# A graph kernel's first hop: the last step's look-ups issued within that step, its matches and marks two tiles a slot, one list step less

## The reference

```python
def _spmm(edge_src, edge_dst, edge_weight, feats, n_nodes):
    msgs = edge_weight[:, None] * feats[edge_src]
    return jax.ops.segment_sum(msgs, edge_dst, num_segments=n_nodes)
feats = [x]; cur = x
for _ in range(n_blocks - 1):            # n_blocks = 4
    cur = _spmm(edge_src, edge_dst, edge_weight, cur, n_nodes)
    feats.append(cur)
gnn = jnp.concatenate(feats, axis=1) @ shared_weight + output_bias
out = _layernorm(x + gnn)                # over the 256 features, eps 1e-5
```

## Time and profile before

| | us |
|---|---|
| three runs of the kernel | 1563.99, 1564.5, 1565.31 (median 1564.5) |
| the profiled execution, its own time | 1565.78 |
| its span on the core | 1563.8 |
| PE busy in the span | 1421.7 (91%) |
| DVE busy | 1193.1 (76%) |
| ACT busy | 1077.0 (69%) |
| POOL busy | 1068.9 (68%) |
| DMA, mean over the span | 286 GB/s |

### The profile page before, as it was taken

The page is one execution under the profiler, slowest core; times in us unless marked ns, Lnnn a source line. Parts: engine busy times, 40 slices in busy tenths (PEclk is TensorE's granted clock), DMA queues, the critical chain, the costliest instruction groups (busy, mean ns, idle before and its releaser), DMA issues. The chain is left out here.

```text
span 1563.8 us, 31224 instructions
## 1 busy us (share of the span) xinstructions
PE 1421.7 (91%) x7970; PEld 1194.6 (76%) x7970; DVE 1193.1 (76%) x4909; ACT 1077.0 (69%) x2674; POOL 1068.9 (68%) x1043
## 2 busy tenths in 40 slices
PE   7999999999999977499989999898889888899993
PEld 5888888888888855388868877777767776677882
DVE  6877777777777768678754443699999999999773
ACT  4777777777777743368855554577777877788774
POOL 4577777777777754657746666357777777777764
PEclk9999999999999989799999999999999999999996
DMA  7889899989998989589978777799999999999862
GB/s 260 280 288 293 294 312 306 304 293 290 308 305 295 308 289 342 178 296 366 369 267 198 172 188 173 226 304 333 321 337 326 336 323 325 335 338 328 298 223 92
DMA packets 221960, 446.52 MB, mean 286 GB/s; under 512 B 30622, under 2 KB 136297, under 8 KB 221787
## 3 DMA queue, kind: packets, MB, share of 16 engines
q1 hardware_dynamic: 171462, 337.11, 62.8%
q0 software_dynamic: 49328, 106.72, 23.4%
q10 hardware_dynamic: 996, 0.72, 0.2%
HBM read 227.00 MB, written 225.94 MB: 290 GB/s over the span
## 5 line engine op out<-in xcount | busy, mean ns | idle before, releaser
L1392 PE MATMUL ps_y<-w_sb,xT 128*128 128x256 f32 x2640 | 696.1, 389 | 26.9 <-DVE y_ring L1716 13.8
L1392 PEld LDWEIGHTS ps_y<-w_sb,xT 128*128 128x128 f32 x2640 | 472.1, 194 | 93.8 <-ACT xT L1104 26.1
L1117 ACT ACTIVATE o_ring<-y_ring,shift,rstd 128x256 f32<-128x256 f32 (+1 forms) x782 | 422.3, 590 | 0.0
L1716 DVE TENSOR_TENSOR y_ring<-ps_y,bias 128x512 f32<-128x512 f32 x391 | 268.5, 687 | 136.9 <-PE ps_y L1392 113.9
L1722 DVE BATCH_NORM_STATS2 stats<-y_ring 128x6 f32<-128x256 f32 (+1 forms) x782 | 290.8, 413 | 3.7
L857 POOL DMA_INDIRECT rows_in<-in_x,gather_idx x200 | 201.3, 1007 | 87.2 <-issue 63.9
L857 POOL DMA_INDIRECT tails_found<-tail_keys,table_idx x200 | 200.2, 1001 | 81.5 <-issue 58.8
L861 POOL DMA_INDIRECT out_rows<-u_out,tailo_idx x197 | 202.2, 1026 | 74.2 <-issue 48.5
L857 POOL DMA_INDIRECT rows_in<-out_rows,tailx_idx x160 | 166.9, 1043 | 84.6 <-issue 37.1
L1476 PE MATMUL ps_u<-w_sb,cT 128*128 128x256 f32 x788 | 206.2, 384 | 0.0
L1381 PE MATMUL ps_xT<-ident,x_ring 128*128 128x128 f32 x1196 | 185.8, 279 | 15.8 <-ACT xT L1104 9.8
(11 more groups left out here) (283 smaller groups left out, 2231.6 us busy)
## 6 DMA issues: line engine op xcount, KB each, us to landing
x_ring<-in_x SPq DMA_DIRECT2D x195, 512.0 KB
out_rows<-o_ring SPq DMA_DIRECT2D x195, 512.0 KB, 4.7
c_rows<-zeros SPq DMA_DIRECT2D x50, 512.0 KB
c_rows<-sums SPq DMA_DIRECT2D x49, 512.0 KB
u_rows<-u_out SPq DMA_DIRECT2D x49, 512.0 KB
keys_bc<-u_rows SPq DMA_DIRECT2D x25, 512.0 KB, 7.1
tails_found<-u_rows SPq DMA_DIRECT2D x12, 512.0 KB, 7.7
listed<-u_rows SPq DMA_DIRECT2D x12, 512.0 KB, 6.6
```

The costliest lines, as they stand in the source:

```text
L1117: last = act.activation(o_ring[slot][0:rows, r * D:(r + 1) * D], y_ring[k][0:rows, r * D:(r + 1) * D], ACT.Identity, bias=shift[k][0:rows, ...
L1392: last = pe.matmul(ps_y[p % 2][0:rows, r * D:(r + 1) * D], columns_of(p)[0][:, q * P:q * P + rows], w_sb[:, c, :], start=c == 0, stop=c == ...
L1716: dve.tensor_tensor(y_ring[k][0:rows, half * 2 * D:(half + 1) * 2 * D], ps_y[half][0:rows, :], bias2[0:rows, :], ALU.add).then_inc(y_copie ...
```

## The change

The look-ups of a-step 24 are issued by POOL within a-step 24, one after each look-up of step 23, and land in buffers of their own (`last_found`, slices of the two key buffers that are free by then), counted on the semaphores `list_in[0]` and `list_in[1]`. For that DVE makes their table index in slot 3 of a-step 24, and ACT counts the tiles of step 24 beside those of step 23, in a-step 23 (two sign operations a slot, none in a-step 24). DVE matches both step 23's and step 24's tiles in list step 0 (two a slot, step 23 in slots 0 to 3), and marks both in list step 1. So `LIST0` is 3 instead of 4: there are nine list steps, and the step behind the head, list step 3, carries two dense units. SP fills four tables of zeros a list step instead of three from list step 1 on; the store of `listed` comes in list step 2, and the rows gathered ahead are stored in list step 3, behind it.

```diff
--- before.py
+++ after.py
@@ -51,11 +51,11 @@
     A_UNIT = STEP
     A_STEPS = TILES // Q
     LIST_UNIT = A_UNIT + PAIR * A_STEPS
-    LIST0 = 4
+    LIST0 = 3
     LIST_STEPS = 5
     LIST_ALL = LIST0 + LIST_STEPS + 1
     ONE = 1
-    B_UNIT = LIST_UNIT + ONE * LIST_ALL + STEP
+    B_UNIT = LIST_UNIT + ONE * LIST_ALL + ONE + STEP
     B_STEPS = LIST_STEPS
     BRIDGE_UNIT = B_UNIT + FOUR * B_STEPS
     FIRST_GROUPS = 2 * LIST_STEPS
@@ -246,6 +246,7 @@
 
         half_keys = [keys_bc[0][:, 0:G * P], keys_bc[0][:, G * P:Q * P], keys_bc[1][:, 0:G * P]]
         half_segments = [t.bitcast(u8)[:, 0:G * P] for t in half_keys]
+        last_found = [keys_bc[1][:, (q + 1) * P:(q + 2) * P] for q in range(Q - 1)] + [keys_bc[0][:, P:2 * P]]
         own_c2 = [u_out[:, k, :] for k in range(G)]
         v_out = [u_out[:, G + k, :] for k in range(G)]
         u_in = [t.rearrange("p (k d) -> p k d", d=D) for t in
@@ -459,7 +460,8 @@
             return A_UNIT + PAIR * i, PAIR, turns, STEP if isinstance(turns, int) and i == 0 else PAIR
 
         def list_step(l):
-            return LIST_UNIT + ONE * l, ONE, 0, PAIR
+            size = [PAIR if i == LIST0 else ONE for i in range(LIST_ALL)]
+            return LIST_UNIT + sum(size[:l]), size[l], 0, size[l - 1] if l > 0 else PAIR
 
         def b_step(b):
             return B_UNIT + FOUR * b, FOUR, 0, FOUR if b > 0 else STEP
@@ -502,7 +504,7 @@
 
         def list_count(m, groups):
 
-            return 16 * G * groups + (16 * G * A_STEPS if m >= 2 else 0)
+            return 16 * G * groups + (16 * G * (A_STEPS - 1) if m >= 2 else 16 * G)
 
         def tile_rows(table, t, n):
 
@@ -639,19 +641,19 @@
                 zero_c2(zeroed + k)
             zeroed += 3
             for l in range(1, LIST_ALL):
-                if l == 2:
+                if l == LIST0 - 1:
+                    sp.wait_ge(listed_copied, A_STEPS)
+                    sp.dma_start(list_dram.rearrange("(p t) f -> p (t f)", p=P),
+                                 listed[:, :, :].rearrange("p t f -> p (t f)")).then_inc(tables_stored, 16)
+                if l == LIST0:
 
                     for k in range(Q):
                         q = (AHEAD0 + k) % Q
                         sp.wait_ge(tailx_in[q], 16)
                         sp.dma_start(ahead_dram[k * P:(k + 1) * P, :], rows_in[q][:, :]).then_inc(rows_ready, 16)
-                if l == LIST0 - 1:
-                    sp.wait_ge(listed_copied, A_STEPS)
-                    sp.dma_start(list_dram.rearrange("(p t) f -> p (t f)", p=P),
-                                 listed[:, :, :].rearrange("p t f -> p (t f)")).then_inc(tables_stored, 16)
                 if l < LIST_ALL - 1:
                     store_and_load(list_step(l))
-                    for k in range(3):
+                    for k in range(4):
                         if zeroed < ZERO_FILLS:
                             zero_c2(zeroed)
                             zeroed += 1
@@ -879,6 +881,12 @@
                 limit(SLOTS)
                 gather(tails_found[:, q, :], tail_keys_dram, table_idx[k][:, q:q + 1], table_done[q // G])
 
+            def look_up_last(q):
+                if q == 0:
+                    pool.wait_ge(table_staged, A_STEPS)
+                    limit(SLOTS)
+                gather(last_found[q], tail_keys_dram, table_idx[(A_STEPS - 1) % 3][:, q:q + 1], list_in[q // G])
+
             def step_a(a, dense, place):
                 last = isinstance(a, int) and a == A_STEPS - 1
                 if isinstance(a, int) and a == 1:
@@ -889,13 +897,13 @@
                         look_up(a - 1, q, (place + 2) % 3)
                     if not last:
                         gather_a(a + 1, q, (place + 1) % 3)
+                    else:
+                        look_up_last(q)
 
             pool.wait_ge(blank, 5)
             for q in range(Q):
                 gather_a(0, q, 0)
             each_a_step(step_a)
-            for q in range(Q):
-                look_up(A_STEPS - 1, q, (A_STEPS - 1) % 3)
 
 
             pool.wait_ge(tables_ready, 2)
@@ -1151,9 +1159,9 @@
                 for q in range(Q):
                     dense_slot(dense, q)
 
-            def count_tiles(a, q):
-
-                last = act.activation(sign_out[q][:, 0:KEYED], first_keys[:, :], ACT.Sign, scale=-1.0,
+            def count_tiles(a, q, compared=sign_out):
+
+                last = act.activation(compared[q][:, 0:KEYED], first_keys[:, :], ACT.Sign, scale=-1.0,
                                       bias=source_key[:, bass.ds(Q * a + q, 1)], accum_out=signs[:, bass.ds(Q * a + q, 1)])
                 if q == Q - 1:
                     last.then_inc(signs_ready, 1)
@@ -1222,7 +1230,10 @@
                     if q % 2 == 1 and e > 2:
                         copy_c1T(e // 2 - 1)
                     dense_slot(dense, q)
-                    count_tiles(a, q)
+                    if a < A_STEPS - 1:
+                        count_tiles(a, q)
+                    if a == A_STEPS - 2:
+                        count_tiles(A_STEPS - 1, q, passed_out)
 
             each_a_step(step_a)
 
@@ -1523,11 +1534,14 @@
                     if l == 0 and q == 0:
                         multiply_u(REAL - 1)
                     if l < LIST0 - 1:
-                        if q == 1:
-                            count_places(A_STEPS + l - 3)
-                        if q >= G:
-                            for k in (2 * (q - G), 2 * (q - G) + 1):
-                                put_in_place(A_STEPS + l - 3, k, (A_STEPS + l - 3) % 3)
+                        if l == 0 and q == 1:
+                            count_places(A_STEPS - 3)
+                        if l == 1 and q % G == 0:
+                            count_places(A_STEPS - 2 + q // G)
+                        if l == 1 or q >= G:
+                            a = A_STEPS - 3 + (0 if l == 0 else 1 + q // G)
+                            for k in (2 * (q % G), 2 * (q % G) + 1):
+                                put_in_place(a, k, a % 3)
                     if l == LIST0 - 1 and q == 0:
                         pe.wait_ge(active_ready, A_STEPS)
                         pe.wait_ge(u_copied, TILES)
@@ -1948,8 +1962,12 @@
 
             def match_tail(a, q):
 
-                dve.wait_ge(table_done[q // G], 16 * G * a + 16 * G)
-                dve.scalar_tensor_tensor(out=match_out[q][:, :], in0=tails_found[:, q, :],
+                last = isinstance(a, int) and a == A_STEPS - 1
+                if last:
+                    dve.wait_ge(list_in[q // G], 16 * G)
+                else:
+                    dve.wait_ge(table_done[q // G], 16 * G * a + 16 * G)
+                dve.scalar_tensor_tensor(out=match_out[q][:, :], in0=last_found[q] if last else tails_found[:, q, :],
                                          scalar=source_key[:, bass.ds(Q * a + q, 1)], in1=place_number[:, :],
                                          op0=ALU.is_equal, op1=ALU.mult, accum_out=place_found[:, q:q + 1]).then_inc(matched, 1)
 
@@ -2027,6 +2045,8 @@
                         copy_listed(a - 4)
                     if q == 1 and (not isinstance(a, int) or a >= 1):
                         stage_look_up(a - 1, (place + 2) % 3)
+                    if q == 3 and last:
+                        stage_look_up(a, place)
                     if q < Q - 2:
                         if e + 2 < REAL:
                             select_a(e + 2, q + 2, place)
@@ -2102,28 +2122,24 @@
                     copy_u(REAL // 2, Q - G, 16 * (A_STEPS - 1))
                 if q == 0:
                     copy_listed(a - 4)
-                if q == 1:
-                    stage_look_up(a - 1, (a - 1) % 3)
                 dense_copy(dense, q)
                 list_slot(a - 3, q)
-                match_tail(a - 2, q)
+                for k in (2 * (q % G), 2 * (q % G) + 1):
+                    match_tail(a - 2 + q // G, k)
                 dense_measure(dense, q)
-            rows_found(a - 2, (a - 2) % 3)
-            dense, a = list_step(1), A_STEPS + 1
+                if q == G - 1:
+                    rows_found(a - 2, (a - 2) % 3)
+            copy_listed(a - 3)
+            find_places(a - 2)
+            rows_found(a - 1, (a - 1) % 3)
+            dense = list_step(1)
             for q in range(Q):
-                if q == 0:
-                    copy_listed(a - 4)
+                if q == G:
+                    copy_listed(a - 2)
+                    find_places(a - 1)
                 dense_copy(dense, q)
-                list_slot(a - 3, q)
-                match_tail(a - 2, q)
-                dense_measure(dense, q)
-            rows_found(a - 2, (a - 2) % 3)
-            dense, a = list_step(2), A_STEPS + 2
-            for q in range(Q):
-                if q == 0:
-                    copy_listed(a - 4)
-                dense_copy(dense, q)
-                list_slot(a - 3, q)
+                for k in (2 * (q % G), 2 * (q % G) + 1):
+                    mark_place(a - 2 + q // G, k)
```

## The result

The changed kernel takes 1570.55 us (median of 20 runs, 1566.08 to 1573.47), the kernel before 1563.92 (20 runs, 1561.03 to 1569.06). The ratio is 1.0034, 95% interval [1.0025, 1.0043]; the same kernel run again gave 1.0039 [1.0024, 1.0053]. The change makes it slower by about 6 us (6.6 between the medians; 5.7 between the means, 1570.4 and 1564.7). The forecast was 1562.8 with 1567.0 as its upper end, so it was wrong, on the side of rival B and 3 us beyond B's own 1567.5. The profiled execution took 1573.25 us, its span is 1571.5.

The account below looks back on a forecast made before the run. It took the side line to last records' copy, then POOL's 44 list gathers, as the bound: wait to 574.4, plus 8.4, 10.6 and 1.0, gives 594.4 against 596.06, 1.7 us less; median 1562.8 us, range 1559.3 to 1567.0.

Parts of the forecast that it names:

- rival B: List step 0: step 23's last look-ups land in 9.3 us and become the late wait; 1567.5 us, chance 0.15.
- ACT's signs, 0.7 us: A-step 23: eight more sign operations make PE wait for ACT's carry, 0.7 us lost; bounds nothing and 3.5.
- Issue and landing of the look-ups: A-step 24 into list step 0: last look-ups issued at 567.5 and 568.8, landing 6.2 us, step 23 in at 574.4.
- Rival A: Look-ups land in 4.9 us, ACT's burst costs nothing, the clock is up; 1559.8 us, chance 0.30.
- The rest of list step 0, 8.4 us: List step 0 behind DVE's wait: remaining matches and records take 8.4 us from 574.4, ending at 582.8.
- 10.6 in all: List step 1 marking both steps: 7.7 us for one plus 2.9 for the second, ending at 593.4.
- I take 1.0: List step 1: allowance of 1.0 us for PE's low clock after its standstill in list step 0.
- the bound of 2.6 us: List step 1: cost on the path if PE's clock is at its low level all the time, 2.6 us.
- With a similar load: List step 1: old list step 2 ran at clock 0.89 with similar load, the reason for taking 1.0 us.
- The head, 7.4 us, unchanged: Between the last records' copy and POOL's first list gather: 7.4 us as before, first gather near 601.8.
- The 44 gathers and everything after shift as a block.: POOL's list and all behind it: gathers of 1.317 us without a gap, moving with the earlier start.
- the forecast's 1.7 less: Whole kernel: copy of the last records at 594.4 against 596.06, so 1.7 us less.

Follow-up runs that it names:

- q2: Kernel before with one edit: step 24's eight sign operations on ACT moved to a-step 23; ratio 1.0001 to the kernel before.
- p1: The changed kernel run again without any edit; ratio 1.0039 to the kernel before.
- s3: The changed kernel again without any edit, for a third trace; no ratio given, first list gather at 603.86 us.
- t1: Changed kernel with six unread filler multiplies on PE ahead of the third hop's first group; ratio 1.0031 to the kernel before.
- q8: Changed kernel with the marks of steps 23 and 24 in one stretch, list step 1's dense unit behind the head; ratio 1.0017 to the kernel before.
- s1: Changed kernel with unread filler multiplies, 16 in slot 4 of list step 0, two per slot of list step 1; ratio 1.0046 to the kernel before.
- p3: Changed kernel with step 24's table index made in slot 1 of a-step 24, waiting only for step 21's look-ups; ratio 1.0012 to the kernel before.
- p4: Changed kernel with the second-half matches of list step 0 moved behind slot 7; ratio 0.9995 to the kernel before.
- p5: Changed kernel with 36 unread filler multiplies on PE in slot 4 of list step 0; ratio 1.0052 to the kernel before.

## Why the prediction was wrong

- *ACT's signs, 0.7 us.* 0.4 us in the traces (one stop, not two), and nothing that the times of q2 can tell.
- *Issue and landing of the look-ups.* Right: last ones at 568.47 and 569.77. The landing took 7.6, 6.1, 7.1 and 6.2 us in the four traces with this front (p1, s3 and t1 beside the first), and the wait ended at 574.65 on average; 574.4 was forecast. Rival A's landing of 4.9 us did not come, nor did rival B's of 9.3: the late wait stands where B put it, but it ends where the forecast had it.
- *The rest of list step 0, 8.4 us.* Right: 8.6, 8.5, 8.6 and 8.5.
- **List step 1, "10.6 in all", and "I take 1.0" for the clock: this step failed.** It measured 13.4, 12.5, 14.2 and 14.6 us, 13.7 on average, 2.1 more than the 11.6. The second round was priced by DVE's own operations (2.9 us). In fact each round is a chain from DVE to PE and back: count, eight puts with a y pair between each two slots, y copy, last marks; 6.0 us at the high clock in p1, of which DVE works 4.0. That is up to 1.4 us (12.0 for 10.6); the rest is the low clock, for which the bound of 2.6 us was about right (14.6 - 12.0) and the 1.0 too little. q8 shows the chain: without the dense work in it both rounds take 5.9 us. "With a similar load" as the old list step 2 was the wrong analogy: PE was busy 6.48 of 7.7 us there and 9.61 of 13.4 at low clock here. The Trainium skill ("TensorE: Matmul & The Clock Gate", Part 1: The HAM clock gate) was the better guide here, by which the slow clock is the default state and activity lifts it; s1, with more work on PE, bears it out with 0.94 against 0.61, though p1's first round had 0.95 without any filler.
- *The head, 7.4 us, unchanged.* 8.7, 7.4, 7.4 and 8.8: it is longer where the clock is low (0.81 in the first trace's window; p3's took 9.7 at 0.53). With this the first list gather is at 604.9 on average, where 601.8 was summed and the kernel before has 603.7.
- **"The 44 gathers and everything after shift as a block."** This failed too. p4 starts the list 6.1 us before the kernel before and is no faster; q8 6.8 us before and is slower. From the first list gather to the end the kernel before needs 961 us (1564.7 - 603.7), the changed one 965.5 (1570.4 - 604.9), p4 967 and q8 971, the first two by the means, the others by the median and the trace's gather. So of the 7.4 us between the forecast's 1.7 less and the measured 5.7 more, 2.9 lie before the list's first gather and 4.5 behind it: this is the larger part of the miss. The work taken out of the first list steps waits behind them: the DMA engines, 0.95 to 0.97 busy from 563.8 to 606 in the four traces with the front of before, are 0.70 to 0.78 busy in the changed one's. That this is what costs the time behind is argued; no run tests it for the changed kernel.

Of the 5.7 us (1570.4 - 1564.7), 1.2 are the later list and 0.4 the second hop, which starts 62.2 us behind it instead of 61.8. Another 0.7 stand behind POOL's last gather (19.3 us to the end, before 18.6, in each of the four traces on either side), and about 1 in the third hop. The rest, 2.4 us, isn't placed in the traces: the four traces with the front of before took 1567.1 us on average, above that kernel's mean of 1564.7, while those with the changed front took 1570.4, just its mean. The clock's mean over the span is 0.9732 in 32 runs of the changed kernel and 0.9767 in 60 of the kernel before, which is 5.6 us of full clock; the window from 563.8 to 606 has a clock of 0.72 on average in the changed kernel's four traces and 0.85 in the four of before, 5.5 us of it. So the list steps hold about as much low clock more as the whole span does. But what of it is time can't be read from the mean: s1 (0.979) and p5 (0.977) have a higher mean clock than the kernel before and are slower than the changed one. The forecast's range, too, ended at 1567.0, half a microsecond short of rival B's own time.

## What to carry to other kernels

A step that two engines pass through in turn is priced by its round trips, not by the busy time of one: draw one round from the trace, with everything that is queued between the two hand-overs, and multiply. Joining two waits into one is dear when independent work stands behind the joined wait; reorder it first. And an earlier start of the bound engine is worth only what the postponed work does not take back behind it.

## What was not expected of the hardware

- TensorE at the low level without a long stop before it: in p5 it was busy without a gap from 565.87 to 581.6 at a clock of 1.00, its longest stop until 588 was 1.25 us, and y pairs went from 0.68 to 1.20 us at 588 all the same, in a stretch in which it worked on and off.
- Two stands at one place of the program, with unlike ends: in the third hop 1.3 us left the clock at 1.00 (p1), 5.1 us brought it to 0.50 for the next 5 us (818 to 823; 0.81 over the stretch), and the stretch took 18.2 instead of 14.0 us.
- The landing of step 23's last look-ups spread over 6.1 to 8.0 us in ten traces, from the same place in the program.
